# Throw-away matmuls beside the first maxima, a maxima store moved between two loads, and two value loads moved to mid-pair

## What is computed

```python
zn  = (z - mu) / jnp.sqrt(var + EPS) * ln_scale + ln_bias        # z is the normalised x, 4 x 1024 x 128
q, k, v = ...                                                   # zn @ w_qkv, 16 heads of 8 channels
scores = jnp.einsum('bhqd,bhkd->bhqk', q, k) / SCALING          # 1024 x 1024 per head
att = jax.nn.softmax(scores, axis=-1)
out = jnp.einsum('bhal,bhlv->bhav', att, v)
s = z + (out @ w_proj + b_proj)
g = silu(ffn(xn))                                               # an RWKV-like channel mix
x = x + s * g
```

## Time and profile before

| | |
|---|---|
| median of 3 runs | 1373.0 us (1372.49 to 1374.38) |
| the profiled execution | 1378.67 us |
| its span, first to last instruction | 1376.6 us |
| PE, DVE, ACT, POOL busy, share of the span | 91%, 73%, 62%, 17% |
| mean granted clock of TensorE, 1.00 = 2.4 GHz | 0.955 |
| first attention, first maxima of its own block to its last value store | 95 to 822 us |
| data moved by DMA | 94.96 MB, mean 69 GB/s |

### The profile page before, as it was taken

The page is one execution under the profiler, slowest core; times in us unless marked ns, Lnnn a source line. Parts: engine busy times, 40 slices in busy tenths (PEclk is TensorE's granted clock), DMA queues, the critical chain, the costliest instruction groups (busy, mean ns, idle before and its releaser), DMA issues. The chain is left out here.

```text
span 1376.6 us, 25966 instructions
## 1 busy us (share of the span) xinstructions
PE 1248.7 (91%) x10305; PEld 578.2 (42%) x10305; DVE 1008.9 (73%) x1288; ACT 852.0 (62%) x1447; POOL 238.3 (17%) x309
## 2 busy tenths in 40 slices
PE   6967999999999999999999978988899799899990
PEld 4631222222221222222222225555599666678870
DVE  5878898998997988998999836664687488523324
ACT  3533888888886888888887875554412366533431
POOL 4200110000000000000000002000286122135560
PEclk9986999999998999999999999998999699999995
DMA  4763123232333223231321112100001111123316
GB/s 143 216 193 73 28 63 70 43 76 51 67 71 74 52 64 73 44 75 44 73 66 46 70 44 76 47 16 16 17 25 45 55 44 36 46 69 101 101 57 187
DMA packets 75205, 94.96 MB, mean 69 GB/s; under 512 B 13237, under 2 KB 44685, under 8 KB 74053
## 3 DMA queue, kind: packets, MB, share of 16 engines
q1 hardware_dynamic: 69996, 83.19, 23.4%
q0 software_dynamic: 5088, 10.12, 2.4%
HBM read 54.30 MB, written 38.56 MB: 67 GB/s over the span
## 5 line engine op out<-in xcount | busy, mean ns | idle before, releaser
L669 ACT ACTIVATE b_exp_ring<-psum 128x512 f32<-128x512 f32 x1024 | 555.5, 599 | 155.2 <-PE psum L724 152.0
L611 DVE TENSOR_REDUCE b_mx<-psum 128x2 f32<-128x1024 f32 x507 | 595.8, 1219 | 72.9 <-PE psum L556 71.8
L724 PE MATMUL psum<-b_q,b_k 75*128 75x512 bf16 x1024 | 313.5, 388 | 5.6 <-DMA b_q<-b_neg 4.1
L700 PE MATMUL psum<-b_exp_ring,b_v 128*32 128x512 f32 x2048 | 275.4, 609 | 0.9 <-ACT b_exp_ring L669 0.7
L724 PEld LDWEIGHTS psum<-b_q,b_k 75*128 75x128 bf16 x1024 | 79.4, 97 | 323.0 <-ACT b_exp_ring L669 221.2
L555 PE MATMUL psum<-b_k,b_q 64*128 64x512 bf16 x512 | 168.8, 395 | 25.7 <-DVE b_mx L611 10.6
L556 PE MATMUL psum<-b_ko,b_qo 64*128 64x512 bf16 x512 | 168.9, 395 | 0.0
L739 POOL CAST b_neg<-b_neg_rest 16x128 bf16<-16x128 f32 x32 | 9.0, 281 | 658.3 <-DVE b_neg_rest L622 658.3
L1831 ACT ACTIVATE e_hT<-psum,e_b 128x358 f32<-128x358 f32 (+3 forms) x96 | 53.7, 561 | 75.3 <-PE psum L1851 72.0
L555 PEld LDWEIGHTS psum<-b_k,b_q 64*128 64x128 bf16 x512 | 44.5, 93 | 128.4 <-issue 41.4
L700 PEld LDWEIGHTS psum<-b_exp_ring,b_v 128*32 128x32 f32 x2048 | 41.3, 108 | 109.1 <-issue 105.6
(11 more groups left out here) (278 smaller groups left out, 1422.9 us busy)
## 6 DMA issues: line engine op xcount, KB each, us to landing
b_q<-q_ops SPq DMA_DIRECT2D x48, 192.0 KB
b_k<-k_ops SPq DMA_DIRECT2D x48, 192.0 KB
k_ops<-a_k SPq DMA_DIRECT2D x20, 256.0 KB, 3.5
x_disp<-b_zeros SPq DMA_DIRECT2D x13, 320.0 KB
e_x<-x_disp SPq DMA_DIRECT2D x8, 520.0 KB
v_ops<-a_vs SPq DMA_DIRECT2D x4, 1024.0 KB, 5.1
b_v<-v_ops SPq DMA_DIRECT2D x16, 256.0 KB
av_out<-b_acc SPq DMA_DIRECT2D x128, 32.0 KB, 1.7
```

What stands on the lines that cost most here:

```text
L611: nc.vector.reduce_max(mx[:, d % 2, :, i // 2, i % 2], pair, AX.X).then_inc(sem("b_max_done"), 1)
L669: act.activation(ex[:, n % E_RING, :], g.bank(5 + n % 3), ACT.Exp, scale=ATT_SCALE)\
L700: last = nc.tensor.matmul(AV[32 * i:32 * i + 32, :], v[s][:, at_v:at_v + 32], ex[:, (4 * group + i) % E_RING, :], start=(kb == 0), stop=(k ...
L724: nc.tensor.matmul(g.bank(5 + n % 3), k[s][0:XROWS, h, kb * P:(kb + 1) * P], q[s][0:XROWS, h, half * BANK:(half + 1) * BANK], start=True, ...
```

## The change

Three edits, all in `layer0_attention`:

- PE's list before the main loop: behind each of the items 5 to 24 come matmuls whose results nobody reads (`busy`), 800 columns behind items 5 to 9, 1900 behind items 10 to 24, and 1900 more after the last. They multiply 64 rows of `b_q` and `b_k` of slot 0 and write PSUM banks 5, 6 and 7, which the main loop uses afterwards. A lot of 800 columns is 2 matmuls (512 and 288), one of 1900 is 4 (three of 512 and one of 364).
- POOL's `load_values`: a wait for `b_av` of 8 x 14 + 2, that is until PE has finished the value products of two key blocks of duo 14, stands ahead of the loads of `d_num` and `d_den`.
- SP's list at the start: `store_maxima(0)` goes between the loads of quad 1 and quad 2 instead of behind both.

```diff
@@ constants
 EARLY = 1
+VALUES_AT = 2
 RECS = B - 1
@@ PE, layer0_attention
             pe.wait_ge(sem("b_rows_set"), SLOTS)
+            def busy(columns):
+
+                for lo in range(0, columns, BANK):
+                    n = min(BANK, columns - lo)
+                    nc.tensor.matmul(g.bank(5 + lo // BANK % 3)[:, 0:n], q[0][0:MROWS, 0, 0:P], k[0][0:MROWS, 0, 0:n],
+                                     start=True, stop=True)
+
             for n in range(FIRST, upto(0, -1)):
                 item(n)
+                busy(800 if n < FIRST + 5 else 1900)
+            busy(1900)
             for d in range(DUOS):
@@ POOL, load_values
                 if b < EARLY:
                     if b:
                         pool.wait_ge(sem("d_oT"), b)
+                    pool.wait_ge(sem("b_av"), TB * (8 * (b + 1) + 6) + VALUES_AT)
                     src = g.av_out[b * 4:b * 4 + 4, :, 0:HD, :].rearrange("q h d t -> (q h) d t")
@@ SP
-            for c in range(1, SLOTS):
+            load_quad(g, sp, 1, 1)
+            store_maxima(0)
+            for c in range(2, SLOTS):
                 load_quad(g, sp, c, c)
-            store_maxima(0)
             sp.wait_ge(sem("b_zeros"), 1)
```

## The result

| | before | after |
|---|---|---|
| median, same chip | 1373.69 us (4 runs) | 1384.31 us (4 runs) |
| ratio | | 1.0082, 95% interval 1.0066 to 1.0098 |
| the profiled execution, its span | 1378.67, 1376.6 us | 1383.43, 1381.4 us |

The change made the kernel 10.6 us slower, where 8.4 us were to be gained. On a second chip the same comparison gave 1384.9 against 1374.14, ratio 1.0078 (1.0062 to 1.0094).

What follows compares the result with a forecast made beforehand. PE was taken to set the pace, losing time to a low clock at the first maxima and to a DMA wait and clock fall at duo 14. 1373.0 - (1.85 + 6.6 = 8.4) = 1364.6 us, range 1362.0 to 1369.8.

Steps and rivals of the forecast that it cites:

- part 2: Throw-away products during the first maxima: clock high before the main loop, gain 3.45 less 1.6 cost, 1.85 us.
- Rival (b): First maxima: clock does not rise, items take 2.0 us, main loop 13.3 us later; 1379.7 us, chance 0.06.
- Part 3: Value loads moved to mid-pair: duo 14 loses its maxima wait and its clock fall, gain 6.6 us.
- Rival (a): Timed runs had no clock fall at duo 14, only the 2.0 us wait; 1369.2 us, chance 0.25.
- Part 1: SP's order at the start: duo 0's maxima rows land by 114.0 us, quad 2's moved loads cost 0.
- early rise: First maxima: clock rises at 101.6 us, so the throw-away products cost 0 and the gain is 3.45 us.
- Rival (c): Throw-away products' weight loads don't hide: items 0.24 us over the beat, 3.6 over 15 items; 1366.5 us, chance 0.06.

Runs made afterwards that it cites:

- twins: Changed kernel, each 64-row throw-away product paired with one on the other 64 rows: 1387.89 against 1396.08 us; also without the two last lots: 1365.82 against 1373.51.

## Why the prediction was wrong

**The step that failed** is in part 2: "The traces give two delays from the start of dense work", 6.8 and 10.1 us, and the choice between them. Both delays were measured in the main loop, where products of 75 rows alternate with value products over the whole array and pairs over both halves. I took any unbroken stream for its equal. The throw-away stream fills the lower 64 rows only, and in three executions of it the clock stayed low for the 37 us that it lasted. Nor is there one delay to be chosen between two: with twins it was 2.7, 2.7, 3.0 and 5.9 us in four executions, with the full-row float32 products 10.2, and from the start of the main loop at the low clock it was 5.6 to 11.9 us in the ten executions that began it low (before, 6.8, is one of them). A delay read from one execution is one draw from such a spread. Rival (b) named this mechanism and its place, with its one piece of evidence, and got 0.06. It priced the item at 2.0 us (measured 2.01) and the start of the main loop at 131.9 (131.10); its 1379.7 is off only by what follows.

**Part 3** was right in its mechanism and in the profile (28.23 to 21.63 us, rows in 1.7 us), but its term, 6.6 us, was mis-sized for the median: the later value loads alone measured 1.8 us, 4.4 at most by the interval. Rival (a) said so, with 2.0. Hence the sum of (b) with (a): 13.3 - 2.0 = +11.3 against +10.6 measured. The two were independent and I gave each a case of its own, never both together; their joint case is 1373.0 + 11.3 = 1384.3.

**Part 1**: the rows land in 1.7 us and the loads of quad 2 disturbed nobody, as said. Its worth alone, 2.1 us in the medians, is not clear of noise, and inside the change it is nothing, because PE is later than the rows. In the kernel before it is worth 2.2 to 2.5 us at the loop's start (116.37 or 116.15 against 118.61), and the spread of the clock's rise is larger than that.

**What was right about the value of a high clock**: 3.45 us were computed for an early rise, 8.4 to 10 with part 3. In the twins' trace key block 2 starts 4.7 us after the loop's first product (117.26 to 121.98), as computed, and duo 14's cast comes at 414.45, 3.85 us ahead of before's 418.30, for a start 0.4 us earlier than the computed 117.7. So this term was right once the clock was up. That the twins gained 8.2 and 7.7 us in all, as much as the forecast, is in part luck: duo 14 gives nearer to 2 than to 6.6. For the 8.2 the traces show where the other 2 to 3 us lie: from duo 15's cast (436.08) to the end this execution takes 949.6 us, the three others profiled on this chip 952.2 to 952.5, with as many matmuls and PE busy for 855 us instead of 858, so less of it at the low clock. That is one execution, and what moved it was not tested.

**Rival (c)**, weight loads that don't hide, did not occur: at the high clock DVE kept its beat with twins, and at the low one the item takes just its columns (2.01 us).

The profile held the evidence for (b): in the rows of the main loop every stream that preceded a rise used more rows than the new one. What weighed too much was that a busy PE and a dense PE look alike in a windows row: 27.00 of 27.00 us here.

## What to carry to other kernels

Throw-away matmuls for the clock are to be built like the work that raised it here, over all 128 rows (two row halves side by side cost no time), and checked by the granted clock in the windows, not by PE's busy time. Size them so that they fit into the beat of the engine that sets the pace at the low clock too, until the rise is certain: 800 columns that failed put the main loop back by 1.8 us here, 1900 by 15. And a gain that one profiled execution shows is only as large in the median as its clock event is frequent; look whether the profile lies above the runs. The time until the clock rises is not a constant to be read from one trace either: here it went from 5.6 to 11.9 us for the same loop.

## What the hardware showed that was not expected

- A stream over 64 rows, PE busy for all of 37 us, left the clock at 1.2 GHz in the three executions profiled with it (the change twice, the products alone once; from 94 to 131 or 132), and with lots of 800 columns for 23 us in a fourth. The same columns over 128 rows brought 2.4 GHz after 2.7 to 5.9 us in four executions. The same half-filled stream kept the high clock for 17 us once it was there (100.0 to 117.2), and pairs in a fifth of the time (0.215 us of 1.14) lost it after 3.5 us.
- The two row halves of the array run ahead of each other. In the changed kernel the upper half's product of an item (L557) starts at 102.10, beside the throw-away products, 1.15 us before the lower half's of the same item (L556, 103.25), although the lower one is first in the program; DVE starts only at 103.93, after the lower one. The Trainium skill, "TensorE: Matmul & The Clock Gate", Part 3, has matmuls strictly in order in start and end; for the starts these rows show otherwise.
- Three small row stores of 4 KB took 6.3 to 6.6 us behind other loads of their own queue (7.2 to 7.6 in the kernel with the later value loads alone) and up to 6.4 beside the value loads of POOL's queue, against 1.7 elsewhere. The Trainium skill, "DMA: Bandwidth & Descriptors", section Queues, rings and completion order, has each engine change between queues packet by packet, which the prediction took to spare the second case. The runs speak against that: once the value loads left later, duo 14's rows landed within 2.9 us in all eleven profiles, within 1.8 in nine of them.
